# Counts, comparison and row differences with the graph halves innermost, in a two-layer graph network on one core

## The reference, cut to what matters

```python
mask = (adj > 0.0)
h  = relu((x @ W1a)[:, :, None, :] + (x[:, :, None, :] - x[:, None, :, :]) @ W1b + b1)
hm = einsum('bjkh,bjk->bjh', h, mask)
x  = layernorm(x + hm @ W2 + deg[..., None] * b2)       # layer 0
m  = relu(relu(x @ W1 + b1) @ W2 + b2)                  # layer 1
msg = relu(adj @ m)
x  = layernorm(x + GRU(msg, x))
```

## Time and profile before

| | |
|---|---|
| time, median of 3 runs | 900.94 us |
| span of the profiled execution | 904.5 us |
| TensorE busy | 823.8 us, 91% |
| VectorE busy | 823.7 us, 91% |
| ScalarE busy | 616.5 us, 68% |
| GpSimd busy | 454.9 us, 50% |
| mean granted TensorE clock | 0.976 |
| L1103 starts at | 11.04, 44.10, 96.98, 148.47, then every 51.4 us until 766.0 |

### The profile page before, as it was taken

One profiled execution on the slowest core, in us unless ns is written; L12 is line 12 of the kernel. 1 busy time (PEld: TensorE's weight loads), 2 busy tenths in 40 slices (PEclk: granted clock), 3 DMA queues, 4 the chain that ended last, 5 costly groups with the idle time before them and its releaser, 6 DMA issues.

```text
span 904.5 us, 25621 instructions
## 1 busy us (share of the span) xinstructions
PE 823.8 (91%) x10240; PEld 565.4 (63%) x10240; DVE 823.7 (91%) x945; ACT 616.5 (68%) x1799; POOL 454.9 (50%) x533
## 2 busy tenths in 40 slices
PE   3778889999999999999999999999999999999973
PEld 2445657666676756666675766667675766666652
DVE  6789999999999999999999999999999999998842
ACT  4534556686876868686786868687786868677641
POOL 4413233564736465473736456473746556353741
PEclk9889999999999999999999999999999999999976
DMA  3331211312130222313131131213122131121000
GB/s 125 88 74 31 71 49 48 83 48 78 49 95 19 61 82 48 93 35 93 48 81 34 49 95 48 78 47 96 27 72 64 49 94 43 48 49 31 1 12 25
DMA packets 31562, 53.34 MB, mean 59 GB/s; under 512 B 8272, under 2 KB 17104, under 8 KB 31440
## 3 DMA queue, kind: packets, MB, share of 16 engines
q1 hardware_dynamic: 31440, 51.67, 21.5%
HBM read 13.90 MB, written 4.19 MB: 20 GB/s over the span
## 4 chain that ended last, share of the span: by engine, by line
PE 63%; issue 17%; DVE 9%; ACT 5%; POOL 4%; DMA 1%; SPq 1%; POOLq 0%; DVEq 0%
PE PS L839 16%; PE PS L848 12%; DVE AC L1177 5%; PE PS L916 3%; POOL AC L1732 2%; PE PS L904 2%; PE PS L825 2%; PE PS L656 2%; PE PS L667 2%; PE PS L926 2%; DVE AC L1157 1%; PE PS L607 1%; PE PS L802 1%; PE PS L616 1%; PE PS L923 1%
## 5 line engine op out<-in xcount | busy, mean ns | idle before, releaser
L1157 DVE SCALAR_TENSOR_TENSOR AC<-PS,AC 128x1152 f32<-128x1152 f32 (+1 forms) x279 | 339.8, 1218 | 19.1 <-PE PS L848 9.6
L1177 DVE SCALAR_TENSOR_TENSOR AC<-PS,AC 128x1152 f32<-128x1152 f32 (+1 forms) x279 | 339.9, 1218 | 15.6 <-PE PS L839 15.2
L839 PE MATMUL PS<-DM,VA 128*128 128x192 fp8e5 (+1 forms) x1152 | 134.6, 240 | 18.1 <-DVE AC L1157 11.5
L839 PE MATMUL PS<-DM,VB 128*128 128x192 fp8e5 (+1 forms) x1152 | 136.5, 242 | 0.8 <-DVE AC L1174 0.8
L1732 POOL TENSOR_TENSOR AC<-AC,NNB 128x512 f32<-128x512 f32 x64 | 66.7, 1061 | 113.0 <-DVE DM L1124 80.9
L848 PE MATMUL PS<-DM,VB 128*64 128x192 fp8e5 (+1 forms) x1152 | 96.5, 246 | 24.3 <-DVE AC L1177 20.8
L839 PEld LDWEIGHTS PS<-DM,VA 128*128 128x128 f16 x1152 | 85.6, 100 | 47.3 <-DVE AC L1157 39.1
L839 PEld LDWEIGHTS PS<-DM,VB 128*128 128x128 f16 x1152 | 76.1, 98 | 38.4 <-DVE AC L1174 1.5
L848 PE MATMUL PS<-DM,VA 128*64 128x192 fp8e5 (+1 forms) x1152 | 98.0, 250 | 0.1
L848 PEld LDWEIGHTS PS<-DM,VB 128*64 128x64 f16 x1152 | 46.5, 109 | 72.7 <-issue 45.8
L1685 POOL TENSOR_SCALAR MT<-AT 128x1024 bf16<-128x1024 f32 x15 | 42.0, 2797 | 60.0 <-DVE DM L1124 52.3
(11 more groups left out here) (263 smaller groups left out, 2001.8 us busy)
## 6 DMA issues: line engine op xcount, KB each, us to landing
CW<-WM SPq DMA_DIRECT2D x128, 160.0 KB, 2.8
AT<-in_adjt SPq DMA_DIRECT2D x16, 512.0 KB, 4.9
VA<-VN SPq DMA_DIRECT2D x64, 96.0 KB, 2.2
VB<-VN SPq DMA_DIRECT2D x64, 96.0 KB, 2.2
XN<-in_xn SPq DMA_DIRECT2D x16, 256.0 KB, 4.9
out<-YO SPq DMA_DIRECT2D x15, 256.0 KB, 2.9
cs<-in_cst SPq DMA_DIRECT2D x1, 545.5 KB, 3.5
out<-YO SPq DMA_DIRECT2D x2, 128.0 KB, 1.7
```

Of the source, the lines that this page charges most:

```text
L839: last = e.matmul(PS[:, b + i % 2, 256 * (i // 2) + cols.start:256 * (i // 2) + cols.stop], lhs[:, GRAPH[i], 0:128], d[:, i, :], start=Fal ...
L1157: e.scalar_tensor_tensor(dst, tiles(PS[:, b:b + 3, :])[:, :, cols], 0.0, dst, ALU.max, ALU.add).then_inc(s["sx"], 1)
L1177: e.scalar_tensor_tensor(dst, tiles(PS[:, b:b + 3, :])[:, :, cols], 0.0, dst, ALU.max, ALU.add).then_inc(s["sy"], 1)
```

## The change

The 16 graph halves become the innermost axis of the comparison. `VE` becomes bf16. `iot` becomes a full tile of 64 row numbers by 16 graph halves, written by GpSimd at the head of `parts`, behind a wait for the constants, with a new semaphore `io` for which VectorE waits before the comparison; VectorE's own copy goes. `SI` is 128 by row number by graph half. L740 reads, for each of 64 row numbers, the 8 halves of its quad (a run of 8 bf16 at a step of 16), and writes PSUM densely in that order. ScalarE reads PSUM at a step of 8 words, so that `OV` has its old layout. L761 reads its 64 elements at a step of 16.

```diff
-        iot = sb("iot", [128, 64], BF16)
+        iot = sb("iot", [128, 64, 2 * GB], BF16)
...
-        VE = sb("VE", [128, NB, 2])
+        VE = sb("VE", [128, NB, 2], BF16)
...
-        SI = [sb(f"SI{i}", [128, GB, 2, 64], BF16) for i in range(2)]
+        SI = [sb(f"SI{i}", [128, 64, 2 * GB], BF16) for i in range(2)]
...
-                e.matmul(PS[:, b, :], shf[:], SI[g % 2][:, c:c + 4, :, :].rearrange("p b k n -> p (b k n)"), start=True,
+                e.matmul(PS[:, b, :].rearrange("p (n m) -> p n m", m=8), shf[:], SI[g % 2][:, :, 2 * c:2 * c + 8], start=True,
                          stop=True).then_inc(s["od"], 1)
...
-                        e.matmul(o, N12[g % 2][:, c + i, h:h + 1].to_broadcast([128, 64]), SI[g % 2][:, c + i, h, :],
+                        e.matmul(o, N12[g % 2][:, c + i, h:h + 1].to_broadcast([128, 64]), SI[g % 2][:, :, 2 * (c + i) + h],
                                  start=False, stop=(i == 3))
...
-                e.tensor_copy(iot[:], cs[:, CIO:CIO + 64])
...
-                io = iot[:].unsqueeze(1).to_broadcast([128, 2 * GB, 64])
+                ends = VE[:, g * GB:(g + 1) * GB, :].rearrange("p b k -> p (b k)")
+                ve.wait_ge(s["io"], 1)
                 ve.wait_ge(s["ve"], g + 1)
                 ve.wait_ge(s["gov"], 2 * (g - 1))
-                e.tensor_tensor(SI[g % 2][:].rearrange("p b k n -> p (b k) n"), io,
-                                VE[:, g * GB:(g + 1) * GB, :].rearrange("p b k -> p (b k)").unsqueeze(2).to_broadcast([128, 2 * GB, 64]),
+                e.tensor_tensor(SI[g % 2][:], iot[:], ends.unsqueeze(1).to_broadcast([128, 64, 2 * GB]),
                                 ALU.is_ge).then_inc(s["ss"], 1)
...
-                e.activation(OV[g % 2][:, c:c + 4, :, :].rearrange("p b k n -> p (b k n)"), PS[:, b, :], ACT.Identity,
+                e.activation(OV[g % 2][:, c:c + 4, :, :].rearrange("p b k n -> p (b k) n"),
+                             PS[:, b, :].rearrange("p (n m) -> p m n", m=8), ACT.Identity,
                              bias=cs[:, CI:CI + 1]).then_inc(s["ov"], 1)
...
             def parts():
+                po.wait_ge(s["dc"], 16)
+                e.tensor_copy(iot[:], cs[:, CIO:CIO + 64].unsqueeze(2).to_broadcast([128, 64, 2 * GB])).then_inc(s["io"], 1)
                 po.wait_ge(s["db"], 32)
```

## The result

The changed kernel takes 905.99 us (median of 15 runs, 903.14 to 908.99); the kernel before takes 901.54 us in the 15 runs made beside them (900.2 to 905.05). The ratio is 1.004, with a 95% interval from 1.0029 to 1.0052: it is slower, by some 4 us, and this is just under the 0.5% (4.5 us) that the prediction counts as a change. The profiled execution spans 904.4 us. That of the kernel before spans 904.5 us, so the two traces agree in their ends, although the medians differ; where the traces part and where they meet again has to be read from the distances between comparisons.

A forecast was written before the change was run, and what follows sets the result against it. TensorE was taken to be what is late at the comparison, though it and VectorE each fill 91% of the span. -0.53 (third octet) - 0.45 (prologue) + 1.7 (L761) = +0.7 us gave 901.6 us, 8-in-10 range 896.5 to 908.5.

The forecast's parts named there:

- The comparison: L1103 on VectorE falls from 1216 to 682 ns, 0.53 us less, worth 0 in the periodic part where TensorE is late.
- The third octet: At 96.98 us the comparison is in the chain, so all 0.53 us of its saving count.
- The prologue: At the first comparison, 0.45 us gained; GpSimd's copy delays VectorE about 1 us, hidden by OV's room.
- the size of L761's read: TensorE's strided read at factor 2: 0.12 us per quad, 14 times, 1.7 us slower.
- one of the prediction's own signs of being wrong: L761 in TensorE's chain taking over 0.1 us a step; 0.06 was the sign of being right.
- The second rival: Slower, as TensorE pays factor 4 on L761 (5.0 us) or L740 doubled (2.7 us); 906.5 us, chance 0.10.
- The forecast's own range: Whole kernel: 899.5 us (L761 free, full prologue gain) to 904 us (prologue at its worst, some of L740).
- the wide one: Whole kernel: the range for 8 in 10, 896.5 to 908.5 us.
- ScalarE's strided read of PSUM: L1459 reads PSUM at a step of 8 fp32 words: taken as 0, bounds 0 and 0.42 us more.
- The first rival: Slower, as ScalarE pays for L1459's strided PSUM read: 5.0 plus 1.3 us, about 908.0 us; chance 0.21.
- VectorE's time counts everywhere: Faster: all 16 comparisons gain 0.53 us each, 8.5 us in sum, 892.4 us; chance 0.11.
- the comparison stays at 1.2 us: L1103 on VectorE gets no shorter and only L761's cost of 1.7 us remains: 902.6 us; chance 0.06.

The follow-up runs named there:

- b_short: The kernel before, with the comparison over one row number in place of 64 from the fifth octet on; 903.98 us, ratio 1.0009.
- b_pairs: The kernel before with its layouts, counts in bf16 written twice side by side and the comparison walking pairs; 901.36 us, ratio 0.9984.
- a_dense: The changed kernel, with L761 reading 64 dense elements of SI (not the right ones); 900.85 us, ratio 0.9987 to the kernel before.
- b_step16: The kernel before, with only L761 reading SI at a step of 16 elements (not the right ones); 907.09 us, ratio 1.0053.
- b_steps: The kernel before, with L761 reading at steps of 2, 4, 8 and 16 elements for a quad's four graphs; 902.96 us, one run.
- b_poolcopy: The kernel before, with only the wait for the constants and the copy of 1024 elements added on GpSimd; 903.02 us, ratio 1.0010.
- b_ov16: The kernel before, with L740 reading 8 rows of 64 single elements at a step of 16; 917.81 us, one run.

## Why the prediction was right or wrong

**The comparison.** 0.68 us was predicted, 681 ns measured. That it is worth nothing in the periodic part held too, within 0.03 us a period, and b_short shows it with twice the saving. The idle time grew by 0.81 us in place of 0.53, since L848 comes 0.3 us later. The Trainium skill ("Vector Engine (DVE) Microarchitecture Reference", Performance modes, on the 2×_1P mode) asks for more than one element innermost, and no more, for the doubled rate; b_pairs agrees, with 681 ns for pairs as for runs of 16.

**The third octet.** Predicted -0.53. From this comparison to the next it takes 50.50 us now and took 51.49 us, 0.99 us less, although L761's read adds 0.17 to 0.24 us there (50.33 us in a_dense; 51.73 us in b_step16 against 51.49). 0.53 us is put down to the comparison: b_steps, which has the long one, has 50.90 us, 0.58 us more than b_pairs, with a little of L761's reads in it. The rest comes from a stretch at half the granted clock, which the kernel before has there and the changed one has not (busy time by stretch; the number before the last two is the granted clock, second line: behind the last octet):

```profile
117.00:125.00 8.00, 6.66 (x67) 4.15 (x64) 7.21 (x9) 0.98 (x2) 2.79 (x1) 0.79 0.04 9
856.01:871.01 15.00, 12.44 (x99) 7.83 (x98) 10.10 (x35) 7.61 (x21) 10.36 (x10) 0.67 0.05 17
```

```profile
115.00:123.00 8.00, 6.25 (x72) 3.83 (x73) 8.00 (x9) 1.53 (x4) 2.79 (x1) 1.00 0.07 17
856.81:871.81 15.00, 12.23 (x105) 7.88 (x104) 10.27 (x36) 7.61 (x22) 10.79 (x10) 0.77 0.05 17
```

Full clock is 2.4 GHz, half is 1.2 GHz. TensorE was waiting often in both: 6.66 and 6.25 us busy of 8. All six traces with the short comparison lack the stretch, with distances of 50.3 to 50.5 us; b_step16, b_short and b_poolcopy have it like the kernel before, with 51.5 to 51.7 us. b_steps and b_ov16 have the long comparison and no such stretch; b_steps' 50.90 us is 0.59 us less than with it, and some of L761's reads are slower in b_steps, so the stretch costs at least that. Behind the last octet the same happens: granted 0.67 before, 0.77 after, 1.00 in a_dense's profiled execution, whose end is 135.4 us after its last comparison, against 138.5 us before and 137.6 us after. These two gains and the slow start of the trace of the kernel before (33.06 us to the second comparison) are why the spans of 904.5 and 904.4 us hide the difference of the medians. What decides whether such a stretch comes is open.

**The prologue.** Predicted -0.45 at 14.60 us; L778 starts at 14.97. The copy took 1.09 us, not 2.8, and L1680 took 0.68 us both times, as predicted. But the copy held VectorE for 0.84 us, as b_poolcopy shows by itself, and the counts that came later met GpSimd's chain. The first comparison is 1.76 us later, OV is ready at 14.18 + 0.69 = 14.87 us and is what L778 now waits for. OV's end moved by 1.22 us, and it had 0.95 us of room; with the counts' part the delay was larger than the 1 us that was taken. The size is not steady, and single traces mislead. Over all twelve, L778 starts at a mean of 14.39 us with the long comparison and no copy on GpSimd (five traces, 14.13 to 14.60), at 13.74 with the short one and no such copy (three, 13.55 to 13.88), at 14.42 with the short one and the copy (three, 14.01 to 14.97), and at 14.81 with the long one and the copy (b_poolcopy). So the gain that was predicted for the shorter comparison is there, 0.65 us, and the copy takes about as much away (0.4 to 0.7 us): about nothing is left where 0.45 us of gain was predicted. The means rest on few traces that scatter by up to 1 us, and the times can't tell it. The Trainium skill ("SBUF — State Buffer", Who interferes with whom) has VectorE blocked outright by a GpSimd instruction when both want the shared pair of ports, not slowed; 0.22 us becoming 1.06 us beside a 1.09 us copy agrees.

**The step that failed: the size of L761's read.** Its place in the chain, its count and the fact that only one quad of a period has it were right. The factor was taken as 2, from fp32 products, and it is 4: 80 ns more for 64 columns of 27 ns. That L761 takes over 0.1 us a step was one of the prediction's own signs of being wrong, and it came. Four steps of 0.12 us, where the kernel before has 0.03, are 0.35 us more in the chain (0.12 was taken), and 0.27 of it reach the period. a_dense, which differs from the changed kernel in this read alone, wins back all but 0.03 us of the 0.35: 616.88 us over the 12 periods against 620.76, 0.32 each. It is 0.05 us a period better than the kernel before, so that much was hidden. TensorE isn't what held it: L848's step in the chain starts 6.60 us after the comparison in both (412.13 us before, 408.30 in a_dense), but the accumulation starts 6.98 us after it before and 6.92 us in a_dense. The nearest reason is that the accumulation at 412.51 had another wait nearly as late, GpSimd's pair of L1732 before, and its counterpart after, in time order:

```profile
410.31 2.07 POOL L1732 TENSOR_TENSOR AC<-AC,NNB 128x512 f32<-128x512 f32 x2 [4.53 <-DVE DM L1124]
```

```profile
408.73 2.06 POOL L1734 TENSOR_TENSOR AC<-AC,NNB 128x512 f32<-128x512 f32 x2 [4.00 <-DVE DM L1123]
```

Before, it ends at 412.38 us, 0.13 us ahead of 412.51; in the changed kernel at 410.79, 0.96 us ahead of 411.75. That this pair was the cause is argued, not shown. With the terms at their measured sizes the sum is 14 x 0.27 = 3.8 us, less 0.5 us at the third octet, and about nothing in the prologue: 3.3 us, where +0.7 was predicted. The medians stood 4.5 us above the kernel before in one set of runs and 1.8 us in another. The second rival had this mechanism, at a chance of 0.10, and 906.5 us. The forecast's own range, to 904, did not hold the 905.99 us; the wide one did. That the result still falls under "same" owes something to luck: the forecast meant +0.7 us, and 4.45 us is the last bit of room under its 4.5.

**ScalarE's strided read of PSUM.** Taken as free, and it is: 687 ns before, after and in a_dense. The first rival, with the largest chance of them, falls. Of the Trainium skill's rule ("Advanced Engine Details and Errata", Memory Cachelines), the SBUF half agrees with L761 and with L740's free runs of 8, except that it takes two elements from a line as enough, while b_steps has factor 2 there (222 ns against 196). The PSUM half speaks of matmuls; ScalarE's read at a step of 8 fp32 words took 687 ns as a dense one did, so it doesn't carry over to it.

**The other rivals.** That VectorE's time counts everywhere is refuted by b_short; that the comparison stays at 1.2 us, by its row.

## What to carry to other kernels

Before a layout is turned for the sake of one VectorE instruction, price every reader of it. Here TensorE's bf16 moving operand took, at the full clock, four times as long per column where each 16-byte line gave one element, twice as long for two, and no longer for four or eight. A broadcast count can be compared at half the time per element by writing it twice in bf16 and walking pairs (681 ns against 1216), and no layout has to turn. And time saved on an engine that then waits for another is idle time: read who ends the idle time behind the instruction first.

## What the runs showed of the hardware

- 64 bf16 moving columns take 196, 222, 274 and 275 ns at steps of 4, 8, 16 and 32 bytes, with 196 ns dense; 512 columns take 389 ns dense or in runs of 8 and 1076 ns singly at 32 bytes.
- ScalarE reads 512 fp32 words of PSUM at a step of 8 words in 687 ns, the same as dense.
- GpSimd's copy and VectorE's L1074 in the same stretch: L1074 took 1.06 us beside the copy and 0.22 us without it (b_poolcopy and before).
- TensorE's granted clock was 0.79 in 117 to 125 us before and 1.00 in 115 to 123 us in the changed kernel, and the distance of the comparisons around it differs by some 0.6 us with and without such a stretch. Behind the last octet it was 0.67 before, 0.77 in the changed kernel and 1.00 in a_dense over 15 us, and the end came 138.5, 137.6 and 135.4 us after the last comparison.
- GpSimd's copy of 1024 elements with a broadcast, fp32 to bf16, took 1.09 us, while its TENSOR_SCALAR of the same size and types in L1685 takes 2797 ns.
